# Six moves in the written-out order of an attention kernel: first set's parts, third batch's statistics, chunk 30's unit, two stores

## The chip, the cores and the metric

The kernel runs on one core of one Trainium2 chip. Its time is device microseconds (us) of one execution; lower is better. Everything is float32 in and out; some products are done in pieces on a faster format (below).

## The reference

Group norm, single-head attention over 1024 positions, projection, residual, for 4 batches:

```python
B, C, H, W = x.shape                          # 4, 128, 32, 32;  N = H*W = 1024
h = _group_norm(x, w, b)                      # 8 groups of 16 channels, over 16 x 1024 values
q = einsum('oc,bcn->bon', qw, h) + qb;  k, v likewise
attn = softmax(einsum('bcn,bcm->bnm', q, k) / sqrt(C), axis=-1)     # 4 x 1024 x 1024
out = einsum('bnm,bcm->bcn', attn, v)
out = einsum('oc,bcn->bon', pw, out) + pb
return x + out
```

## The kernel before

The weights of query and key are multiplied once (`wa`), and so are those of value and projection (`wpv`). A batch then needs one projection `g` of the normalised input `h` (`project_g`, two halves), the scores g against h, and value tiles `v` with the projection already in them (`value_tiles`, three groups of 3, 3 and 2 tiles). Products of large weight are split into a rounded part and a remainder (`h_hi`, `h_lo`, `g_hi`, `g_lo`, `p_hi`, `p_lo`, `v_hi`, `v_lo`) and summed from three matmuls.

The queries are 32 **chunks** of 128, eight for each batch. One loop over c = 0 to 31 (a **step** each) is written out on every engine, and each engine works through its own list in order, held back by semaphores alone.

- TensorE (PE) in step c: `scores(c)` into one of two PSUM halves; then the steps' extras; then `value_unit(c - 8)`, a quarter of the work of an older set.
- VectorE (DVE): `drain_scores(c)` takes the scores out of PSUM (L804), then `transpose_blocks(c - 1)` (L813).
- ScalarE (ACT): `exponentials(c)` (L620), with copies and roundings ahead of it and behind it.
- GpSimd (POOL): the remainders `v_lo` (L969), `p_lo` (L976), `h_lo`, biases and residuals.
- SyncE (SP) issues the DMAs: `move_set(n)` is 16 DMAs that carry a set's 32x32 blocks to their places in `pT`; `spread_rows(n)` spreads the softmax denominators; `store_set(n)` writes results.

Chunks form nine **sets** (`SETS = 2, 4, 4, 4, 4, 4, 4, 4, 2`); set 6 is chunks 22 to 25, set 7 is 26 to 29. Sets 1 to 7 go through the move, and their value work is a unit per chunk number: unit m of set n is `moved_unit`. Those in `SPLIT_UNITS` run as three matmuls of 256 columns per tile on `p_hi` and `p_lo` (L442 to L444), so they wait for ACT's `round_probs` (L638) and POOL's `split_probs` (L976). The first set (chunks 0, 1) and the last (30, 31) are transposed on PE instead (`transpose_probs`, L498), copied out as `pair_T` by ACT and DVE, and need no move. The first set's value work is four parts (`first_set_part`, L412), each in the step that `FIRST_SET_STEPS` names. Chunks 30 and 31 have a unit each, `last_chunk_unit` (L423).

The statistics of batch 2 (the third) are made on the way: ACT sums (`channel_means`, L592 to L595, after the exponentials of step 6; `channel_squares`, L599 to L602, after those of step 7) and raises `chan_ready`. Then PE multiplies by the deviation matrix (`group_deviations`, L303), DVE makes `cvar` and `neg_mean` (`channel_vars`, L752 and L753), PE averages (`group_vars`, L308), DVE makes `gvar` (`group_var`, L759), and POOL goes on from there. `turn_rden(1)` in step 10 (L396) waits for that `gvar`, since both use the PSUM bank A0. In steps 8 to 10 PE's lists are:

```python
# step 8:  scores(8), value_tiles(1, 1), group_deviations(2)
# step 9:  scores(9), project_g(1, 1), group_vars(2), first_set_part(3)
# step 10: scores(10), value_tiles(1, 2), turn_rden(1), value_unit(2)
```

ACT in step 10: `copy_v(1, 2)` (L610, waits for `value_tiles(1, 2)`), `copy_rows(1)`, `exponentials(10)`, then `round_probs` for units (1,2) and (1,3), that is units 4 and 5. PE reaches unit 4 in step 12.

After the loop PE's list is units 24, the transposes of chunk 31, unit 25, two `broadcast_rden`, units 26, 27, chunk 30's unit, units 28, 29, chunk 31's unit. Every unit raises `part_done` by one, and DVE's closing operations wait for counts of it. SP's list in its last rounds is move 6, spread 6, store 4, move 7, store 5, store 6, then chunk 30, set 7, chunk 31.

Of the kernel before, what the change touches and what calls it, by code (L numbers as in the profile page):

```python
# [18 lines left out]

SETS = (2, 4, 4, 4, 4, 4, 4, 4, 2)  # L20

FIRST_SET_STEPS = (4, 5, 6, 9)
FIRST_DIVIDED = 11
LAG = 8

TURN_STEPS = (3, 10, 11, 15, 19, 23, 27)
ROW_STEPS = (4, 10, 12, 15, 20, 23, 28)

DEVIATION_STEPS = (0, 8, 16)
VARIANCE_STEPS = (1, 9, 17)  # L30

CHANNEL_STEPS = (6, 7)

# [5 lines left out]
def build(nc, x, vectors, weights, out):  # L39
# [28 lines left out]
    with ExitStack() as ctx:  # L68
# [158 lines left out]
        def unit_end(r):  # L227

            n, u = SPLIT_UNITS[r]
            return FIRST[n] + u + 1  # L230

        def blocks_view(n):
            return blocks[:, n % 2, 0:SETS[n] * N].rearrange("p (j t c q) -> p j t c q", j=NQ, t=KT, c=SETS[n])
# [3 lines left out]
        @block.sync  # L237
        def _(sp):
            def move_set(n):
                sp.wait_ge(blocks_ready, FIRST[n + 1] - SETS[0])  # L240
                if n == 2:
                    sp.wait_ge(chan_ready, 3)
                if n > 2:
                    sp.wait_ge(part_done, FIRST[n - 1])
                for a in range(NQ):
                    for j in range(NQ):
                        sp.dma_start(moved_view(n)[Q * j:Q * (j + 1), a].rearrange("p t n -> p (t n)"),
                                     blocks_view(n)[Q * a:Q * (a + 1), j].rearrange("p t c q -> p (t c q)"))\
                          .then_inc(moved[n % 2][a], 16)

            def spread_rows(n):
                sp.wait_ge(rows_stored[n % 2], 16 * (n // 2 + 1))
                if n > 1:
                    sp.wait_ge(out_ready, n - 1)
                sp.dma_start(rden_bc[:, n % 2, 0:P * SETS[n]], row_store[n:n + 1, 0:P * SETS[n]].to_broadcast([P, P * SETS[n]]))\
                  .then_inc(rows_spread[n % 2], 16)

            def store_set(n):
                if n < SPREAD_BY_DMA:
                    sp.wait_ge(out_ready, n + 1)  # L260
                else:
                    sp.wait_ge(tail_out_ready, 3)
                at = P * FIRST[n]
                while at < P * (FIRST[n] + SETS[n]):
                    b, first = at // N, at % N
                    width = min(N, first + P * (FIRST[n] + SETS[n]) - at) - first
                    sp.dma_start(out[b, :, first:first + width], xb[:, b, first:first + width]).then_inc(stored, 16)
                    at += width

            def store_chunk(d):  # L270
                sp.wait_ge(tail_out_ready, (2, 4)[d])
                cs = slice(P * (CH - 2 + d), P * (CH - 1 + d))
                sp.dma_start(out[L, :, cs], xb[:, L, cs]).then_inc(stored, 16)

            for f in range(HALVES):
                cs = slice(BANK * f, BANK * (f + 1))
                sp.dma_start(x_sb[:, 0, cs], x[0, :, cs]).then_inc(x0_loaded[f], 16)
            sp.wait_ge(x0_loaded[0], 16)
            sp.dma_start(x_sb[:, 1, :], x[1]).then_inc(x1_loaded, 16)
            sp.dma_start(x_sb[:, 2:B, :], x[2:B].rearrange("b c n -> c b n")).then_inc(xs_loaded, 16)  # L280
            spread_rows(0)
            move_set(1)
            spread_rows(1)
            for n in range(2, LS):
                move_set(n)
                if n < SPREAD_BY_DMA:
                    spread_rows(n)
                store_set(n - 2)
            store_set(LS - 2)
            store_chunk(0)  # L290
            store_set(LS - 1)
            store_chunk(1)
            sp.wait_ge(stored, 16 * (NS + 1 + sum(crosses(n) for n in range(NS))))

        @block.tensor
        def _(pe):
# [119 lines left out]

            def last_chunk_unit(d):
                for f in range(HALVES):
                    pe.wait_ge(pair_ready[f], SETS[0] + SETS[LS])
                pe.wait_ge(v_ready, VP * B)  # L420
                pe.wait_ge(rowmin_ready, STEPS)
                for t in range(KT):
                    last = pe.matmul(chunk_sums[d], v[:, L % 3, t, :], pair_T[:, t, d, :], start=(t == 0), stop=(t == KT - 1))  # L423
                last.then_inc(part_done, 1)
# [89 lines left out]
            for c in range(STEPS):  # L514
                b, i = c // CH, c % CH

                late = i - 1 if b == 0 else i
                scores(c)
                if c == DEVIATION_STEPS[0]:
                    group_deviations(1)  # L520
                if late == 0:
                    value_tiles(b, 1)
                if late == 1:
                    project_g(b, 1)
                if late == 2:
                    value_tiles(b, 2)
                if c in DEVIATION_STEPS[1:]:
                    group_deviations(DEVIATION_STEPS.index(c) + 1)
                if c in VARIANCE_STEPS:
                    group_vars(VARIANCE_STEPS.index(c) + 1)  # L530
                if c in TURN_STEPS:
                    turn_rden(TURN_STEPS.index(c))
                if i == 6 and b < L:
                    project_g(b + 1, 0)
                if i == 7 and b < L:
                    value_tiles(b + 1, 0)
                if c - 2 in range(SETS[0]):
                    transpose_probs(c - 2)
                if c > DIRECT:
                    transpose_probs(c - 1)  # L540
                if c in FIRST_SET_STEPS:
                    first_set_part(FIRST_SET_STEPS.index(c))
                if c >= LAG + SETS[0]:
                    value_unit(c - LAG)
            value_unit(STEPS - LAG)
            transpose_probs(STEPS - 1)
            for m in range(STEPS - LAG + 1, FIRST[LS - 1]):
# [2 lines left out]
            broadcast_rden(LS)  # L550
            value_unit(FIRST[LS - 1])
            value_unit(FIRST[LS - 1] + 1)
            value_unit(DIRECT)
            value_unit(FIRST[LS - 1] + 2)
            value_unit(FIRST[LS - 1] + 3)
            value_unit(DIRECT + 1)
# [173 lines left out]
        def _(dve):  # L730
# [89 lines left out]
                dve.reciprocal(rden[:, n % 2, 0:SETS[n]], den[:, n % 2, 0:SETS[n]]).then_inc(rden_ready, 1)  # L820

            def divide(n):
                dve.wait_ge(part_done, FIRST[n] + SETS[n])
                if n < SPREAD_BY_DMA:
                    dve.wait_ge(rows_spread[n % 2], 16 * (n // 2 + 1))
                else:
                    dve.wait_ge(bc_ready, n - SPREAD_BY_DMA + 1)
                by_rden = rden_bc[:, n % 2, 0:P * SETS[n]]
                if n == 0:
                    dve.tensor_tensor(by_rden, sums[n], by_rden, ALU.mult).then_inc(normed_ready, 1)  # L830
                else:
                    by_rden = by_rden.rearrange("p (c a q) -> p a c q", c=SETS[n], a=NQ)
                    dve.tensor_tensor(by_rden, sums[n].rearrange("p (a c q) -> p a c q", a=NQ, c=SETS[n]), by_rden, ALU.mult)\
                       .then_inc(normed_ready, 1)

            def finish_last_chunk(d):
                dve.wait_ge(part_done, (STEPS - 3, STEPS)[d])
                dve.wait_ge(bc_ready, 2)
                by_rden = rden_bc[:, LS % 2, P * d:P * (d + 1)]
                dve.tensor_tensor(by_rden, chunk_sums[d], by_rden, ALU.mult).then_inc(chunk_normed, 1)  # L840
                dve.wait_ge(chunk_normed, d + 1)
                dve.wait_ge(xb_ready, B)
                xs = xb_flat[:, P * (DIRECT + d):P * (DIRECT + d + 1)]
                dve.tensor_tensor(xs, by_rden, xs, ALU.add).then_inc(tail_out_ready, 1)

            def finish_last_moved(part):
                n = LS - 1
                dve.wait_ge(part_done, FIRST[n] + 2 if part == 0 else STEPS - 1)
                dve.wait_ge(bc_ready, 1)
                by_rden = rden_bc[:, n % 2, 0:P * GC].rearrange("p (c a q) -> p a c q", c=GC, a=NQ)[:, 2 * part:2 * (part + 1)]  # L850
                dve.tensor_tensor(by_rden, last_sums[part].rearrange("p (a c q) -> p a c q", a=2, c=GC), by_rden, ALU.mult)\
                   .then_inc(last_normed, 1)
                dve.wait_ge(last_normed, part + 1)
                dve.wait_ge(xb_ready, B)
                xs = xb_flat[:, columns(n)].rearrange("p (c a q) -> p a c q", c=GC, a=NQ)[:, 2 * part:2 * (part + 1)]
                dve.tensor_tensor(xs, by_rden, xs, ALU.add).then_inc(tail_out_ready, 1)
# [34 lines left out]
            for c in range(STEPS):  # L891
                b, i = c // CH, c % CH
                late = i - 1 if b == 0 else i
                if c - 1 in DEVIATION_STEPS:
                    channel_vars(DEVIATION_STEPS.index(c - 1) + 1)
                if c - 1 in VARIANCE_STEPS:
                    group_var(VARIANCE_STEPS.index(c - 1) + 1)
                if i == 3 and b < L:
# [150 lines left out]
```

## Time and profile before

| what | value |
|---|---|
| median of 3 runs | 134.87 us (134.65 to 138.57) |
| the profiled execution, its own time | 134.62 us |
| its span, first to last instruction | 132.9 us |
| PE busy | 124.7 us, 94% of the span |
| DVE, ACT, POOL busy | 98.6 (74%), 84.9 (64%), 69.7 us (52%) |
| chain that ended last, share of PE | 80% |

The span is what the trace shows; the 1.7 us between it and the execution's own time lie outside the instructions. A row of the timeline gives start, duration, engine, line and operation, and in brackets how long the engine stood idle before it and what ended that. Matmuls overlap: the next starts some 0.1 to 0.2 us before the last one's record ends, so lengths of work on PE are read best from start to start.

### The profile page before, as it was taken

How to read it: one execution, taken by the hardware profiler on the slowest of the kernel's cores; microseconds unless marked ns; L12 is line 12 of the kernel's file. 1: busy time of each engine (PE TensorE's matmuls, PEld its weight loads, DVE VectorE, ACT ScalarE, POOL GpSimd, SP SyncE). 2: the span in 40 equal slices, each digit the busy share in tenths (PEclk: the TensorE clock that was granted, in tenths of full speed). 3: DMA queues.
4: the chain of work that ended last, by engine and by line, in shares of the span. 5: the costliest groups of instructions: out<-in, count | busy, mean ns of one | idle time of the engine just before them, and what ended most of it. 6: DMA issues, size and time to landing. Idle time of an engine off the chain costs nothing.

```text
span 132.9 us, 2364 instructions
## 1 busy us (share of the span) xinstructions
PE 124.7 (94%) x767; PEld 110.2 (83%) x767; DVE 98.6 (74%) x159; ACT 84.9 (64%) x149; POOL 69.7 (52%) x51
## 2 busy tenths in 40 slices
PE   5899999998699999999999999999999999699991
PEld 5897887886587889999898888898888999698991
DVE  0577878999969878989699999756987898130421
ACT  4055588768967996968756999678595369412000
POOL 5044015950006798696656696866749329923000
PEclk9999999999999999999999999999999999999999
DMA  4970000023896398899684898699738896897502
GB/s 129 286 297 0 0 5 0 0 42 81 201 215 138 122 213 205 190 239 213 167 195 125 199 215 185 198 215 222 184 142 197 204 210 221 197 212 165 178 20 99
DMA packets 9712, 21.01 MB, mean 158 GB/s; under 512 B 2378, under 2 KB 4196, under 8 KB 9700
## 3 DMA queue, kind: packets, MB, share of 16 engines
q1 hardware_dynamic: 8960, 20.59, 61.4%
q10 hardware_dynamic: 740, 0.28, 0.8%
q8 instruction: 6, 0.10, 0.3%
q14 instruction: 6, 0.05, 0.1%
HBM read 4.07 MB, written 2.11 MB: 46 GB/s over the span
## 4 chain that ended last, share of the span: by engine, by line
PE 80%; issue 6%; DVE 4%; DMA 3%; ACT 2%; POOL 2%; SPq 0%; POOLq 0%
PE ACC L471 16%; PE S L384 10%; PE S L385 9%; PE S L388 9%; PE ACC L442 6%; PE A L364 5%; PE ACC L444 5%; PE ACC L443 5%; PE S L423 3%; DMA x_sb<-x 3%; PE S L328 2%; POOL p_lo L976 2%; PE ACC L412 2%; DVE s_sb L804 1%; PE ACC L498 1%
## 5 line engine op out<-in xcount | busy, mean ns | idle before, releaser
L804 DVE TENSOR_SCALAR_CACHE_REDUCE s_sb<-S,row_term 128x1024 f32<-128x1024 f32 x32 | 40.9, 1278 | 12.3 <-PE S L388 12.0
L620 ACT ACTIVATE s_sb<-s_sb,rowmin 128x1024 f32<-128x1024 f32 x32 | 36.9, 1154 | 11.1 <-DVE s_sb L804 9.0
L976 POOL TENSOR_TENSOR p_lo<-pT,p_hi 128x1024 fp32r<-128x1024 f32 x14 | 33.4, 2394 | 11.5 <-ACT p_hi L638 11.5
L813 DVE STREAM_TRANSPOSE blocks<-s_sb 128x1024 f32<-128x1024 f32 x28 | 34.7, 1240 | 0.3
L384 PE MATMUL S<-h_hi,g_hi 128*128 128x512 f32 x64 | 27.7, 433 | 0.3 <-issue 0.3
L471 PE MATMUL ACC<-pT,v 128*128 128x128 f32 (+1 forms) x160 | 26.5, 317 | 0.0
L385 PE MATMUL S<-h_lo,g_hi 128*128 128x512 f32 x64 | 25.1, 393 | 0.0
L471 PEld LDWEIGHTS ACC<-pT,v 128*128 128x128 f32 x160 | 23.1, 191 | 2.1
L388 PE MATMUL S<-h_hi,g_lo 128*128 128x512 f32 x64 | 19.8, 391 | 0.0
L442 PE MATMUL ACC<-p_hi,v_hi 128*128 128x256 f32 x56 | 16.4, 293 | 1.2 <-POOL p_lo L976 1.1
L443 PE MATMUL ACC<-p_lo,v_hi 128*128 128x256 f32 x56 | 15.7, 281 | 0.0
L444 PE MATMUL ACC<-p_hi,v_lo 128*128 128x256 f32 x56 | 15.7, 281 | 0.0
L638 ACT CAST p_hi<-pT 128x1024 fp32r<-128x1024 f32 x14 | 14.4, 1039 | 1.3 <-DMA pT<-blocks 1.1
L388 PEld LDWEIGHTS S<-h_hi,g_lo 128*128 128x128 f32 x64 | 12.0, 188 | 2.8
L939 POOL TENSOR_TENSOR rstd<-gvar,minus_half 128x1 f32<-128x1 f32 x4 | 2.2, 553 | 22.5 <-DVE gvar L759 22.5
L384 PEld LDWEIGHTS S<-h_hi,g_hi 128*128 128x128 f32 x64 | 12.1, 189 | 2.0 <-issue 0.5
L969 POOL TENSOR_TENSOR v_lo<-v,v_hi 128x1024 fp32r<-128x1024 f32 x4 | 9.5, 2384 | 7.9 <-ACT v_hi L628 7.9
L385 PEld LDWEIGHTS S<-h_lo,g_hi 128*128 128x128 f32 x64 | 12.1, 189 | 1.6
L442 PEld LDWEIGHTS ACC<-p_hi,v_hi 128*128 128x128 f32 x56 | 10.5, 188 | 2.0 <-issue 1.7
L443 PEld LDWEIGHTS ACC<-p_lo,v_hi 128*128 128x128 f32 x56 | 10.6, 189 | 0.3
L444 PEld LDWEIGHTS ACC<-p_hi,v_lo 128*128 128x128 f32 x56 | 10.6, 189 | 0.0
L364 PEld LDWEIGHTS A<-wpv,h 128*128 128x128 f32 x64 | 8.6, 190 | 2.4 <-issue 1.7
(110 smaller groups left out, 172.5 us busy)
## 6 DMA issues: line engine op xcount, KB each, us to landing
pT<-blocks SPq DMA_DIRECT2D x112, 128.0 KB, 2.4
rden_bc<-row_store SPq DMA_DIRECT2D x6, 256.0 KB, 3.7
x_sb<-x SPq DMA_DIRECT2D x1, 1024.0 KB, 5.9
out<-xb SPq DMA_DIRECT2D x4, 256.0 KB, 3.1
out<-xb SPq DMA_DIRECT2D x7, 128.0 KB, 3.0
x_sb<-x SPq DMA_DIRECT2D x2, 256.0 KB, 3.0
x_sb<-x SPq DMA_DIRECT2D x1, 512.0 KB, 3.8
w_in<-weights ACTq DMA_DIRECT2D x2, 128.0 KB, 3.6
```

The costliest lines, as they stand in the source:

```text
L364: last = pe.matmul(A1[:, PW1 * u:PW1 * (u + 1)], h[:, P * t:P * (t + 1)], wpv[:, 0:PW1], start=True, stop=True)
L384: pe.matmul(S[:, c % 2, ks], g_hi[:, qs], h_hi[:, b % 2, ks], start=True, stop=False)
L385: pe.matmul(S[:, c % 2, ks], g_hi[:, qs], h_lo[:, b % 2, ks], start=False, stop=False)
L388: last = pe.matmul(S[:, c % 2, ks], g_lo[:, qs], h_hi[:, b % 2, ks], start=False, stop=True)
L442: pe.matmul(to, v_hi[:, t, :], p_hi[:, r % 2, w, :], start=(t == 0), stop=False)
L443: pe.matmul(to, v_hi[:, t, :], p_lo[:, r % 2, w, :], start=False, stop=False)
L444: last = pe.matmul(to, v_lo[:, t, :], p_hi[:, r % 2, w, :], start=False, stop=(t == KT - 1))
L471: last = pe.matmul(to, v[:, b % 3, t, :], probs[:, :, t, :], start=(t == 0), stop=(t == KT - 1))
L620: act.activation(s_sb[:, c % 3, :], s_sb[:, c % 3, :], ACT.Exp, bias=rowmin[:, c % CH:c % CH + 1], scale=-1.0, accum_out=den[:, n % 2, k:k ...
L804: dve.tensor_scalar(s_sb[:, c % 3, :], S[:, c % 2, :], row_term[:, b % 2, i:i + 1], None, ALU.add, ALU.min, accum_out=rowmin[:, i:i + 1]). ...
L813: dve.transpose(blocks_view(n)[:, :, :, k, :].rearrange("p j t q -> p t j q"), s_sb[:, c % 3, :].rearrange("p (t j q) -> p t j q", t=KT, j ...
L976: pool.tensor_tensor(lo, probs, hi.bitcast(F32), ALU.subtract).then_inc(p_lo_ready, 1)
```

## The change

- `FIRST_SET_STEPS` goes from (4, 5, 6, 9) to (5, 6, 7, 9). In step 7 `value_tiles(1, 0)` now stands behind that step's part.
- `group_deviations(2)` goes from the end of step 8 to just behind `scores(9)`; its `group_vars(2)` goes behind the first set's last part in step 9. DVE's `channel_vars` keeps its steps through a constant of its own. In step 10 `value_tiles(1, 2)` goes behind `value_unit(2)`.
- Chunk 30's unit goes ahead of unit 24. It now waits for three copied pairs instead of all four, and the counts of `part_done` behind it are adjusted.
- Stores 4 and 5 are issued behind move 7.

```diff
-FIRST_SET_STEPS = (4, 5, 6, 9)
+FIRST_SET_STEPS = (5, 6, 7, 9)
-DEVIATION_STEPS = (0, 8, 16)
+DEVIATION_STEPS = (0, 9, 16)
+CHANNEL_VAR_STEPS = (1, 9, 17)
...
-            return FIRST[n] + u + 1
+            return FIRST[n] + u + (2 if FIRST[n] + u >= STEPS - LAG else 1)
...
-                store_set(n - 2)
-            store_set(LS - 2)
+                if n < LS - 2:
+                    store_set(n - 2)
+            for n in range(LS - 4, LS - 1):
+                store_set(n)
...
-                    pe.wait_ge(pair_ready[f], SETS[0] + SETS[LS])
+                    pe.wait_ge(pair_ready[f], SETS[0] + d + 1)
...
                 scores(c)
-                if c == DEVIATION_STEPS[0]:
-                    group_deviations(1)
+                if c in DEVIATION_STEPS[:2]:
+                    group_deviations(DEVIATION_STEPS.index(c) + 1)
...
-                if late == 2:
+                if late == 2 and b != 1:
                     value_tiles(b, 2)
-                if c in DEVIATION_STEPS[1:]:
-                    group_deviations(DEVIATION_STEPS.index(c) + 1)
-                if c in VARIANCE_STEPS:
+                if c == DEVIATION_STEPS[2]:
+                    group_deviations(3)
+                if c in VARIANCE_STEPS and b != 1:
                     group_vars(VARIANCE_STEPS.index(c) + 1)
...
-                if i == 7 and b < L:
+                if i == 7 and 0 < b < L:
                     value_tiles(b + 1, 0)
...
                     first_set_part(FIRST_SET_STEPS.index(c))
+                if i == 7 and b == 0:
+                    value_tiles(1, 0)
+                if c == VARIANCE_STEPS[1]:
+                    group_vars(2)
                 if c >= LAG + SETS[0]:
                     value_unit(c - LAG)
+                if late == 2 and b == 1:
+                    value_tiles(1, 2)
+            value_unit(DIRECT)
             value_unit(STEPS - LAG)
...
-            value_unit(DIRECT)
             value_unit(FIRST[LS - 1] + 2)
...
-                dve.wait_ge(part_done, FIRST[n] + SETS[n])
+                dve.wait_ge(part_done, FIRST[n] + SETS[n] + (1 if n == LS - 2 else 0))
-                dve.wait_ge(part_done, (STEPS - 3, STEPS)[d])
+                dve.wait_ge(part_done, (STEPS - LAG + 1, STEPS)[d])
-                dve.wait_ge(part_done, FIRST[n] + 2 if part == 0 else STEPS - 1)
+                dve.wait_ge(part_done, FIRST[n] + 3 if part == 0 else STEPS - 1)
```

## Rows read from the trace of the kernel before

**Rows 1.** The page, TensorE's granted clock in 40 slices of the span

```profile
PEclk9999999999999999999999999999999999999999
```

**Rows 2.** Timeline of PE, steps 4 to 12: start, us, engine, line, operation

```profile
23.45 1.10 PE L412 MATMUL ACC<-pair_T,v 128*128 128x256 f32 x4 [0.38 <-issue]
...
31.58 0.91 PE L364 MATMUL A<-wpv,h 128*128 128x129 f32 x6 [0.47 <-DVE g_lo L786]
...
33.71 0.83 PE L364 MATMUL A<-wpv,h 128*128 128x129 f32 x6
35.71 0.38 PE L303 MATMUL A<-chan,deviation 128*128 128x1 f32 x2 [1.17 <-ACT chan L602]
35.95 0.48 PE L384 MATMUL S<-h_hi,g_hi 128*128 128x512 f32 x1
...
37.41 0.40 PE L340 MATMUL A<-h_hi,wa_hi 128*128 128x512 f32 x1
...
40.84 0.68 PE L364 MATMUL A<-wpv,h 128*128 128x129 f32 x4
41.36 0.27 PE L396 MATMUL A<-ident,rden 128*4 128x128 f32 x1
41.47 1.89 PE L471 MATMUL ACC<-pT,v 128*128 128x256 f32 x8
43.01 0.58 PE L384 MATMUL S<-h_hi,g_hi 128*128 128x512 f32 x1
...
47.82 0.28 PE L442 MATMUL ACC<-p_hi,v_hi 128*128 128x256 f32 x1
```

**Rows 3.** Timeline of DVE, steps 5 to 10

```profile
25.95 1.28 DVE L804 TENSOR_SCALAR_CACHE_REDUCE s_sb<-S,row_term 128x1024 f32<-128x1024 f32 x1 [0.19 <-PE S L388]
...
36.28 0.18 DVE L752 SCALAR_TENSOR_TENSOR cvar<-A,chan 128x1 f32<-128x1 f32 x1
...
37.61 1.28 DVE L804 TENSOR_SCALAR_CACHE_REDUCE s_sb<-S,row_term 128x1024 f32<-128x1024 f32 x1 [1.08 <-PE S L388]
...
40.61 0.14 DVE L759 TENSOR_SCALAR gvar<-A 128x1 f32<-128x1 f32 x1
```

**Rows 4.** Timeline of ACT, steps 7 to 10

```profile
35.45 0.20 ACT L602 ACTIVATE chan<-chan_sums 128x1 f32<-128x1 f32 x1
...
41.56 0.37 ACT L610 COPY v<-A 128x256 f32<-128x256 f32 x1 [0.44 <-PE A L364]
...
43.78 1.98 ACT L638 CAST p_hi<-pT 128x1024 fp32r<-128x1024 f32 x2
```

**Rows 5.** Timeline of POOL, units 4 and 5, and units 24 and 25

```profile
44.89 4.75 POOL L976 TENSOR_TENSOR p_lo<-pT,p_hi 128x1024 fp32r<-128x1024 f32 x2 [0.90 <-ACT p_hi L638]
...
112.53 4.70 POOL L976 TENSOR_TENSOR p_lo<-pT,p_hi 128x1024 fp32r<-128x1024 f32 x2
```

**Rows 6.** Timeline of PE, behind the loop

```profile
111.99 1.95 PE L471 MATMUL ACC<-pT,v 128*128 128x128 f32 x16
115.04 0.36 PE L442 MATMUL ACC<-p_hi,v_hi 128*128 128x256 f32 x1 [1.10 <-POOL p_lo L976]
...
123.00 1.95 PE L423 MATMUL S<-pair_T,v 128*128 128x128 f32 x16
124.78 3.62 PE L471 MATMUL ACC<-pT,v 128*128 128x256 f32 x16
```

**Rows 7.** Timeline of ACT, the copy of chunk 30's pair

```profile
112.65 0.58 ACT L660 COPY pair_T<-A 128x512 f32<-128x512 f32 x1
```

**Rows 8.** Timeline of SP: start, length of issuing, line

```profile
30.76 10.12 SPq L247 DMA_DIRECT2D pT<-blocks  x16
...
110.77 11.25 SPq L247 DMA_DIRECT2D pT<-blocks  x16
122.06 1.58 SPq L267 DMA_DIRECT2D out<-xb  x3
```

**Rows 9.** Issues by line, set moves from 108 us on: us from issue to landing

```profile
DMA to landing us min/median/max: 2.3/2.7/3.2
```

More of the change, by code:

```diff
@@ L893, in _ @@
                 late = i - 1 if b == 0 else i
-                if c - 1 in DEVIATION_STEPS:
-                    channel_vars(DEVIATION_STEPS.index(c - 1) + 1)
+                if c in CHANNEL_VAR_STEPS:
+                    channel_vars(CHANNEL_VAR_STEPS.index(c) + 1)
                 if c - 1 in VARIANCE_STEPS:
```

## The prediction

> **What bounds the kernel now.** I read the busy times first: TensorE is busy 124.7 of 132.9 us, and the chain that ended last is 80% its own. So an edit pays only where TensorE stands still, and only if the time isn't given back at its next wait. The second view is therefore TensorE's timeline with the brackets. It has four places that the edits touch. In step 4 the first set's first part waits 0.38 us. In step 7 the value tiles of batch 1 wait 0.47 us for DVE's `g_lo`. In step 8 the deviation product waits 1.17 us for ACT's `chan` [rows 2]. Behind the loop unit 24 waits 1.10 us for POOL's `p_lo` [rows 6]. Between unit 4 in step 12 and the end of the loop TensorE goes from one operation to the next nearly without a bracket. So I treat the kernel as a front (to unit 4 at 47.82 us), a middle of fixed length, and a tail. The third view is the timelines of DVE, ACT and POOL, to see what feeds unit 4 and what else is late in the tail.
>
> **Part 1, the front: parts a step later, deviations behind scores 9.** The question is when unit 4 starts, and the answer needs two chains: when TensorE gets there, and when `p_lo` gets there.
>
> Steps 4 to 7. Without a part in step 4, scores 5 ends earlier, and DVE's drain of step 5 loses its idle 0.19 us [rows 3], with the handover some 0.25. From there DVE drains and transposes without pause until `g_lo`, so the value tiles of step 7, which wait for that `g_lo`, start 0.25 earlier: 31.58 becomes 31.33 [rows 2]. TensorE, which no longer loses 0.38 in step 4, simply waits longer here (about 1.1 us instead of 0.47). Moving the parts thus yields 0.25 us, not 0.38 + 0.47.
>
> Steps 8 and 9. The second value tiles start at 33.71 and are recorded for 0.83; less the 0.17 by which a follower overlaps (part 2) they take 0.66, to 34.37; then comes the wait, and scores 9 start at 35.95 [rows 2]. Now scores 9 follow the tiles at once: 34.37 - 0.25 = 34.12. They take 37.41 - 35.95 = 1.46 [rows 2], so the deviation product can start at 35.6. `chan` is written at 35.65 [rows 4] and rides on the same copy and exponential as before, so it comes 0.25 earlier, at 35.4. The wait is gone. DVE is free for `cvar` at 36.28 - 0.25 = 36.03, as before less the 0.25, and behind it stands drain 9, queued after the added wait. In the kernel before this drain waited 1.08 us for scores 9 [rows 3]. That idle time goes, since scores 9 end before `cvar` is even made; drain 9 starts at about 36.3 instead of 37.61, 1.3 earlier. The drain, a transpose and `g_lo` lead on to `gvar`, so `gvar` starts at 40.61 - 1.3 = 39.3 [rows 3] and is done at 39.45. The cost of the product between scores 9 and the projection is a tenth of a microsecond and lies in DVE's shadow.
>
> Step 10. TensorE is done with scores 10 before that, and `turn_rden` waits for `gvar` with nothing in front of it any more. From `gvar` to the start of `p_lo` of unit 4 the sum goes: handover 0.1; the turn 41.47 - 41.36 = 0.11; unit 2, now ahead of the tiles, 43.01 - 41.47 = 1.54 [rows 2]; from the start of the last two value tiles to their copy on ACT 41.56 - 40.84 = 0.72 [rows 2, 4]; from that copy through the rows and the exponential to the rounding, 43.78 - 41.56 = 2.22 [rows 4]; from the rounding to `p_lo` 44.89 - 43.78 = 1.11 [rows 4, 5]. That is 5.80, so `p_lo` starts at 45.25. From the start of a `p_lo` to the start of its unit takes 115.04 - 112.53 = 2.51 [rows 5, 6]. Unit 4 can start at **47.76, against 47.82 before**: the reorder makes `gvar` 1.3 earlier, and it puts unit 2 (1.54) between `gvar` and the exponential on ACT, which is queued behind the copy of those tiles.
>
> TensorE itself gets there earlier: scores 11 would start at 39.45 + 0.1 + 0.11 + 1.54 + 0.45 (two tiles, two thirds of the 0.66) = 41.65 instead of 43.01, and 4.81 later [rows 2], at 46.5, it stands before unit 4 and waits 1.3 us. So nearly all that the front wins is paid back at one new wait, which no bracket of the present trace shows because POOL is just in time. Unit 5 follows: its `p_lo` is done 4.75 us after 45.25, at 50.0, and the unit starts a unit and a pass of scores behind unit 4, 3.0 us by the lengths above, at 50.8, which leaves 0.8. Net for the front: 0.06 us, bounds from +0.4 (handovers) to -1.3 (unit 4 is not held back at all).
>
> **A rule against this new wait.** The trace grants the full level, 2.4 GHz, in every slice, though TensorE stands still for 1.17 and 1.10 us in it [rows 1, 2, 6]. The Trainium skill says that TensorE's clock is gated by default and activity releases it ("TensorE: Matmul & The Clock Gate", What's actually happening); it would let four waits in steps 7 to 12, the longest 1.3 us, end at 1.2 GHz. The mechanism would be a stretch at half rate behind the wait. A pair of scores and unit is 1.46 + 1.54 = 3.0 us here [rows 2], so one such pair at half rate adds 3.0.
>
> **Part 2, the tail: chunk 30's unit ahead of unit 24.** The unit is only moved, so TensorE's work stays the same and it fills the wait. Unit 23 starts at 111.99 and is recorded for 1.95; a follower starts 0.17 before such an end (123.00 + 1.95 against 124.78), so at 113.77 [rows 6]. What the moved unit needs is there: ACT's copy ends at 113.23 [rows 7], DVE's beside it at the same time, and DVE's copy stands in its list behind the drain of the last scores. It takes 124.78 - 123.00 = 1.78, to 115.55; unit 24 starts 0.51 later than 115.04 and all that followed chunk 30's old place 1.78 - 0.51 = **1.27 us earlier** [rows 6]. The `p_lo` of unit 25 is done at 117.23 [rows 5], ahead of the unit's 117.9. DVE finishes chunk 30 between the two halves of set 7, with time in hand.
>
> What is late next is set 7's move. Unit 28 needs the last quarter of it; it would be asked for at 124.78 - 1.27 - 0.06 = 123.45. The move starts when chunk 29's blocks are made, at 110.77, and is issued in 11.25 us here, 10.12 in the first [rows 8]. Its last DMA lands 2.3 to 2.7 us after its issue [rows 9], which itself lies 0.6 before the end. That gives 122.6 to 124.1. I take no wait, nearer to the shorter end, since the stores no longer go ahead of this move and only issues held up for a microsecond make the long case; the long end costs 0.65.
>
> **Part 3, the two stores.** Store 4 is two DMAs ahead of move 7, about 1.05 us by the 1.58 for three [rows 8]; I count nothing for taking it away, since move 7 has a condition of its own, the blocks of chunk 29. Had the store held it up, the move would start up to 1.05 earlier, which only takes chance from rival (b). Behind the move stand five store DMAs instead of three; three take 1.58 [rows 8], so five take 2.6 and end near 124, while chunk 30's store is wanted at about 125 and the last near 129.6. At nothing, as long as SP stays that far ahead; if not, the last store would slip by 0.4 a DMA.
>
> **Sum.** -0.06 - 1.27 = -1.33 us. The profiled execution goes from 134.62 to 133.3, and the median, 0.25 above it, from 134.87 to 133.5. The change of `unit_end` and the other counts follow the new order and cost nothing.
>
> **The rivals.** (a) The front is kept: unit 4 isn't held by `p_lo`, because ACT's list catches up in its idle time. For it speaks that ACT and POOL are busy only 64% and 52%; against it, that the chain above has no slack in it. It gives 133.5 - 1.3 = 132.2. (b) The last move isn't in time, and unit 28 waits up to 0.65: 134.2. For it speaks the 11.25. (c) Slower than before: the tiles behind unit 2 cost more than the statistics win. Every tenth that `gvar` comes later than 39.45 delays unit 4 by a tenth, and the middle hands it on to the end. The point from which it decides is a `gvar` at 40.8: from there on the tail's 1.27 is used up. If `chan` comes so late that DVE's drain 9, now queued behind `cvar`, gains nothing, and the 0.6 of round trip to TensorE and back is added, `gvar` is 1.9 later: 133.5 + 1.9 = 135.4. Against it: `chan` comes from ACT's own list, which nothing in steps 5 to 8 delays. (d) The clock falls for one pair: 133.5 + 3.0 = 136.5; against it the full clock after every present wait [rows 1]. (e) The tail does nothing, since its unit isn't ready when unit 23 ends: 134.8; the copies' ends half a microsecond before speak against it.
>
> **How the numbers follow.** The forecast, 133.0 to 134.0, has 0.62; (a) 0.12; (b) 0.12; (c) 0.08; (d) 0.02; (e) 0.04. The likeliest gives 133.5. The range leaves out most of (c), (d), and a corner of the others: 132.1 to 134.9. Two per cent, about what a measurement of this kernel tells from no change, is 2.7 us, so below 132.17 counts as faster: a part of (a), 0.05. Slower begins at 137.57, beyond (d) on average: 0.01. Within lies 0.94.
>
> **What the profile after would show.** Brackets at 23.45 and before L303 gone; a longer one before L364 in step 7; one of about 0.4 before L396 in step 10; `gvar` near 39.4; a bracket of about 1.3 before L442 near 47.8, ended by POOL's `p_lo`; chunk 30's unit (L423) near 113.7, with no bracket before unit 24; unit 28 near 123.4. I am wrong if unit 4 starts more than half a microsecond away from 47.8, or if unit 28 or unit 24 has a bracket of its own.

## The result, and the profile after

The changed kernel takes 134.03 us (median of 18 runs, 133.5 to 138.0) against 134.85 us in as many runs of the kernel before. The ratio is 0.9949, 95% interval 0.9937 to 0.9960, so the change makes the kernel 0.7 us faster, 0.5%; that is clear of no change, and under the two per cent that the prediction took as faster. (Medians are over all runs, 0.8 us apart here; ratios, here and below, leave out the few runs that took some 3% longer, such as the 138.0.) The forecast was 133.5 us, 1.33 us faster. The profiled execution took 134.02 us, its span is 132.3 us, and TensorE is busy for 124.9 us of it, 0.2 more than before. The clock row is again full in every slice.

TensorE's timeline of the changed kernel, the front, with the rows that answer to [rows 2] (lines have moved by four on TensorE, ten on DVE, ACT and POOL, and two on SP):

```profile
24.28 1.02 PE L416 MATMUL ACC<-pair_T,v 128*128 128x256 f32 x4
...
31.28 0.91 PE L368 MATMUL A<-wpv,h 128*128 128x129 f32 x6 [0.77 <-DVE g_lo L796]
...
34.01 0.47 PE L388 MATMUL S<-h_hi,g_hi 128*128 128x512 f32 x1
...
35.49 0.31 PE L307 MATMUL A<-chan,deviation 128*128 128x1 f32 x2
...
39.41 0.27 PE L400 MATMUL A<-ident,rden 128*4 128x128 f32 x1
39.53 1.96 PE L475 MATMUL ACC<-pT,v 128*128 128x256 f32 x8
41.34 0.61 PE L368 MATMUL A<-wpv,h 128*128 128x129 f32 x4
...
47.83 0.36 PE L446 MATMUL ACC<-p_hi,v_hi 128*128 128x256 f32 x1 [1.27 <-POOL p_lo L986]
```

The waits of steps 4 and 8 are gone; scores 9 start at 34.01 instead of 35.95. The wait of step 7 has grown from 0.47 to 0.77 in its bracket, and step 9 has a small one of 0.20 before its projection. The last row holds the bracket of 1.27 us that was not there before, and unit 4 starts at 47.83 where it started at 47.82.

What comes between, on DVE, ACT and POOL of the changed kernel ([rows 3], [rows 4] and [rows 5] answer to these):

```profile
36.00 0.18 DVE L762 SCALAR_TENSOR_TENSOR cvar<-A,chan 128x1 f32<-128x1 f32 x1
...
39.16 0.15 DVE L769 TENSOR_SCALAR gvar<-A 128x1 f32<-128x1 f32 x1
```

```profile
41.98 0.37 ACT L620 COPY v<-A 128x256 f32<-128x256 f32 x1 [2.25 <-PE A L368]
...
44.20 1.98 ACT L648 CAST p_hi<-pT 128x1024 fp32r<-128x1024 f32 x2
```

```profile
45.30 4.75 POOL L986 TENSOR_TENSOR p_lo<-pT,p_hi 128x1024 fp32r<-128x1024 f32 x2 [2.76 <-ACT p_hi L648]
```

`gvar` is 1.45 us earlier than before (39.16 against 40.61), but ACT then stands idle for 2.25 us until the last value tiles come, and the rounding and `p_lo` are 0.4 later than before.

TensorE's timeline behind the loop ([rows 6]) and SP's ([rows 8]), changed kernel:

```profile
112.05 1.95 PE L475 MATMUL ACC<-pT,v 128*128 128x128 f32 x16
113.83 1.95 PE L427 MATMUL S<-pair_T,v 128*128 128x128 f32 x16
115.54 0.36 PE L446 MATMUL ACC<-p_hi,v_hi 128*128 128x256 f32 x1
...
119.99 3.62 PE L475 MATMUL ACC<-pT,v 128*128 128x256 f32 x16
124.15 3.69 PE L475 MATMUL ACC<-pT,v 128*128 128x256 f32 x16 [0.54 <-DMA pT<-blocks]
127.68 1.95 PE L427 MATMUL S<-pair_T,v 128*128 128x128 f32 x16
```

```profile
110.82 11.33 SPq L249 DMA_DIRECT2D pT<-blocks  x16
122.20 2.57 SPq L269 DMA_DIRECT2D out<-xb  x5
125.09 0.33 SPq L275 DMA_DIRECT2D out<-xb  x1
128.79 0.33 SPq L269 DMA_DIRECT2D out<-xb  x1
130.31 0.33 SPq L275 DMA_DIRECT2D out<-xb  x1
```

Chunk 30's unit fills the wait ahead of unit 24, which has no bracket any more. But unit 28 stands until 124.15 for the last quarter of set 7's move; without that it would follow unit 26 by 3.46 us, the time from unit 26 to the next operation in [rows 6] (119.54 to 123.00), at 123.45. That is 0.70 of the 1.27 us given back. SP is done issuing that move at 110.82 + 11.33 = 122.15, and unit 28 starts 2.00 us later. The five stores are issued by 124.8, before chunk 30's is wanted.

### The profile page after: what moved, and what is told of

Its sections match the earlier page's. It is cut to its first block, busy times and chain, and to the rows that moved or that the text cites. A ratio compares the mean times of both kernels' runs of the same rounds, so it can differ in the third digit from the quotient of the medians.

```text
span 132.3 us, 2364 instructions
## 1 busy us (share of the span) xinstructions
PE 124.9 (94%) x767; PEld 110.3 (83%) x767; DVE 98.3 (74%) x159; ACT 84.6 (64%) x149; POOL 69.9 (53%) x51
## 4 chain that ended last, share of the span: by engine, by line
PE 70%; SPq 8%; DVE 7%; issue 6%; ACT 3%; POOL 2%; DMA 2%; ACTq 0%; POOLq 0%; DVEq 0%
PE ACC L475 12%; PE S L388 9%; PE S L389 8%; PE S L392 8%; SPq L249 8%; PE A L368 6%; PE S L332 5%; PE ACC L446 4%; PE ACC L448 4%; PE ACC L447 4%; DVE blocks L823 3%; DVE s_sb L814 2%; DMA pT<-blocks 2%; POOL p_lo L986 2%; PE S L427 1%
```

## The experiments

The theory (A) was the prediction's, with rival (b) (set 7's move isn't in time) now seen to have come true: the front gives nothing net because the value tiles behind unit 2 hold `p_lo` of unit 4; the tail gives 1.3 less what unit 28 waits. The runs of one group shared a chip.

**Part alone: the tail.** The kernel before with chunk 30's unit moved, with its shorter wait and the counts that go with it.

```diff
+            value_unit(DIRECT)
             value_unit(STEPS - LAG)
...
             value_unit(FIRST[LS - 1] + 1)
-            value_unit(DIRECT)
```

> The kernel before with one part of the change: chunk 30's unit ahead of unit 24, and the counts that go with it. Theory A (the front gives nothing net, the tail gives all): 0.6 us faster than before, ratio 0.995 to 0.996, the whole change's; unit 24 without a bracket near 115.5 us, and unit 28 waiting about 0.6 us for the last quarter of set 7's move. Rival B (the front does give something that the tail loses again): 0.3 us or less, ratio above 0.9975.

Measured: 133.83 us, ratio 0.9917 (0.9896 to 0.9938). A's 0.995 to 0.996 lies outside that: the gain is 1.1 us and not 0.6, and no smaller than the whole change's. TensorE's closing rows show why:

```profile
113.80 1.95 PE L423 MATMUL S<-pair_T,v 128*128 128x128 f32 x16
115.51 0.36 PE L442 MATMUL ACC<-p_hi,v_hi 128*128 128x256 f32 x1
...
119.97 7.37 PE L471 MATMUL ACC<-pT,v 128*128 128x256 f32 x32
127.18 1.95 PE L423 MATMUL S<-pair_T,v 128*128 128x128 f32 x16
```

Units 26 to 29 run in one group here with no bracket. They take 127.18 - 119.97 = 7.21 us, only 0.29 more than the 2 x 3.46 that they need; in the changed kernel they take 7.69. The move was issued in 10.89 us instead of 11.33. SP is done with it at 121.69, and unit 28 starts 1.97 us later, at 123.66. So the gain of the tail stands, and its loss depends on the move.

**Part alone: the front.** The changed kernel with the tail and the stores put back.

> The changed kernel with chunk 30's unit and the two stores put back: the front's reorder alone. Theory A: no difference, ratio 0.999 to 1.001; TensorE waits 1.3 us before unit 4, which starts at 47.8 us, and 1.1 us again before unit 24. Rival B: 0.3 to 0.6 us faster, ratio below 0.998.

Measured: 134.97 us, ratio 1.0000 (0.9982 to 1.0018), as A had it. TensorE waits 1.3 us before unit 4 and 1.1 before unit 24, 2.4 us together. In this profile all times behind the first scores are 0.4 us late (those start at 12.13 instead of 11.72 us); from there to unit 4 (48.22) it is 36.09 us, against 36.10 before.

**The stores back.** `store_set(n - 2)` in every round of SP's loop again, the rest as changed.

> The changed kernel with stores 4 and 5 back in their old places. Theory A (the stores neither hold nor slow set 7's move; its length comes from one DMA whose issuing is held up by a microsecond, which happens either way): the same as the changed kernel, 0.6 to 0.7 us faster than before. Rival C (two DMAs ahead of the move slow its first issues): unit 28 starts 0.4 us later, ratio 0.998.

Measured: 134.08 us, ratio 0.9946 (0.9925 to 0.9967): the same as the changed kernel. Rival C's 0.998 lies outside, and moving the stores does nothing that can be measured. Only store 4 changes its place at all: store 5 stood behind move 7 in the kernel before too, as the first of the three DMAs at 122.06 in [rows 8]. The profiled execution was the slowest of its ten (134.84 us); unit 28 waited 1.10 us in it, and its move has this DMA:

```profile
L249 SPq DMA_DIRECT2D pT<-blocks x1: 2194/2194/2194, 118.9 to 118.9; - x1
```

It is one issue of 2.19 us, where nearly all others take 0.59; another of this move takes 0.80.

**The value tiles back.** The changed kernel, with the last two tiles of batch 1 ahead of the turn and unit 2, as they were.

```diff
-                if late == 2 and b != 1:
+                if late == 2:
                     value_tiles(b, 2)
...
-                if late == 2 and b == 1:
-                    value_tiles(1, 2)
```

> The changed kernel with the last two value tiles of batch 1 back ahead of the turn and unit 2 in step 10. Theory A (those tiles behind unit 2 hold ACT's exponential of step 10, and with it the p_lo of unit 4, which gives back all that the statistics win): ACT copies the tiles near 40.0 instead of 41.98 us, p_lo of unit 4 starts at 44.0 instead of 45.30 (by then the move of set 1 is the next limit), unit 4 starts at 46.4 to 46.6 and the bracket before it falls under 0.3 us; the middle carries it to the end, 1.2 to 1.4 us faster than the changed kernel, ratio to before 0.985 to 0.987. Rival D (POOL or the move of set 1 holds unit 4 anyway): 0.5 us or less faster than the changed kernel, ratio above 0.991.

Measured: 132.86 us, ratio 0.9841 (0.9811 to 0.9870): 1.2 us faster than the changed kernel by the medians, 1.4 to 1.5 by the ratios. Its ACT, POOL and TensorE:

```profile
40.32 0.37 ACT L618 COPY v<-A 128x256 f32<-128x256 f32 x1 [0.38 <-PE A L368]
...
42.80 2.00 ACT L646 CAST p_hi<-pT 128x1024 fp32r<-128x1024 f32 x2 [0.16 <-DMA pT<-blocks]
```

```profile
43.92 4.77 POOL L984 TENSOR_TENSOR p_lo<-pT,p_hi 128x1024 fp32r<-128x1024 f32 x2 [1.17 <-ACT p_hi L646]
```

```profile
46.59 0.28 PE L446 MATMUL ACC<-p_hi,v_hi 128*128 128x256 f32 x1
```

Where the two tiles stand accounts for the front's loss. ACT's idle time goes from 2.25 to 0.38 us, `p_lo` starts at 43.92 (expected 44.0), and unit 4 has no bracket. The rounding now waits 0.16 us for set 1's move, but TensorE doesn't wait for it. Rival D is out.

**The changed kernel again**, as the reference of the second group.

> The changed kernel once more, beside the next three on one chip, so that small differences can be read against it. Theory A: ratio to before 0.992 to 0.996, with times spread over half a microsecond or more, since how long one held-up DMA of set 7's move takes differs from run to run and unit 28 waits for it.

Measured: 134.21 us, ratio 0.9937 (0.9909 to 0.9965), as A had it; eight of the nine times lie between 133.42 and 134.45. Unit 28 has a bracket of 0.54 again, and the tenth DMA of the move is issued in 1.97 us.

**The last rows behind unit 27.** The two `broadcast_rden` after units 26 and 27.

> The changed kernel with the six transposes that broadcast the last denominators behind units 26 and 27 instead of ahead of them. TensorE's work is the same; 0.65 us of it moves into the place where unit 28 waits for the last quarter of set 7's move. Theory A (what the tail lacks of its 1.3 us is that DMA's landing): unit 28 starts as before with no bracket or under 0.3 us, 0.3 to 0.6 us faster than the changed kernel. Rival E (something else behind unit 28 sets the end, the stores behind the move or DVE's closing work): no difference.

Measured: 134.13 us, ratio 0.9919 (0.9888 to 0.9949), not told apart from the changed kernel. The expectation was reasoned wrongly: the rows stood ahead of unit 28 already, so nothing was moved into its wait. What the run does show is that unit 28 starts at nearly the same time in either order ahead of it:

```profile
119.45 3.69 PE L475 MATMUL ACC<-pT,v 128*128 128x256 f32 x16
122.98 0.82 PE L406 MATMUL S<-ident,rden 128*128 128x128 f32 x6
124.27 3.69 PE L475 MATMUL ACC<-pT,v 128*128 128x256 f32 x16 [0.47 <-DMA pT<-blocks]
```

Units 26 and 27 come 0.7 us earlier than in the run beside it, and unit 28 at 124.27 instead of 124.33. So set 7's move sets its start. Whether something behind unit 28 holds the end as well (rival E) it doesn't decide.

**Part alone: the first set's parts.** The kernel before with `FIRST_SET_STEPS = (5, 6, 7, 9)` and step 7's value tiles behind the part.

> The kernel before with the first set's parts a step later and the value tiles of step 7 behind that step's part, and nothing else. Theory A: the wait of step 4 goes and the one of step 7 grows; DVE comes 0.25 us earlier and so does everything up to unit 4, since the reorder of step 10 isn't in it: 0.2 to 0.3 us faster than before, ratio 0.998. Rival F (the parts alone are worth the brackets that they remove, 0.38 and 0.47): 0.8 us faster, ratio 0.994. Rival G: nothing, ratio 1.000.

Measured: 134.61 us, ratio 0.9971 (0.9953 to 0.9990): about 0.4 us faster, in the direction of A; A's 0.998 lies in the interval, rivals F and G outside it. The wait of step 7 is 0.77 us, `gvar` starts at 40.38 instead of 40.61, and unit 4 at 47.58 instead of 47.82. So the trace bears out 0.24 at unit 4, but not at the end: TensorE is still 0.25 ahead at 94.98, the next unit's `p_lo` starts at 93.73 (92.95 before), and at 96.29 TensorE is 0.02 behind (96.27 before). The span is 132.9 us in both profiles, so what of the 0.4 us is the parts' isn't shown.

**Both repairs.** Tiles back and the rows behind unit 27.

> Both repairs: the value tiles of step 10 back ahead of unit 2, and the last denominators' transposes behind unit 27. Theory A: the two waits are in series on TensorE, so the gains add: 1.5 to 1.9 us faster than the changed kernel, about 132.4 us, ratio to before 0.981 to 0.984; no bracket of more than 0.3 us between step 8 and the last unit.

Measured: 132.10 us, ratio 0.9781 (0.9754 to 0.9809), faster than A's 0.981 to 0.984. The interval lies just below those of both runs with the tiles alone (0.9841, and 0.9834 below), so the second repair may add something here. It isn't shown, since those ran on other chips and the profiles end alike: the last unit starts at 125.59 here and at 125.54 in the second run with the tiles alone. No bracket of over 0.3 us stands between step 8 and the end. Its held-up DMA is 1.34 us, and the move 10.76.

**The last quarter issued from ACT.** Behind `exponentials(31)` in ACT's list.

```diff
-                for a in range(NQ):
+                for a in range(NQ - 1 if n == LS - 1 else NQ):
...
                 exponentials(c)
+                if c == STEPS - 1:
+                    act.wait_ge(blocks_ready, FIRST[LS] - SETS[0])
+                    act.wait_ge(part_done, FIRST[LS - 2])
+                    for j in range(NQ):
+                        act.dma_start(moved_view(LS - 1)[Q * j:Q * (j + 1), NQ - 1].rearrange("p t n -> p (t n)"), ...)
```

> The changed kernel with the last four of set 7's sixteen move DMAs issued from ACT, behind its last exponential near 114.5 us, in place of SP. Theory A (unit 28 waits for the end of a row of DMAs whose length is their issuing, sixteen of 0.63 us and one held up for a microsecond more): SP is done with its twelve near 119.7, the last quarter lands before 120.5, unit 28 has no bracket and starts at 123.45; 0.4 to 0.7 us faster than the changed kernel, ratio to before 0.989 to 0.991. Rival H (the transfers themselves are the limit, so that two queues only share them): the last of them lands no earlier than 123, the bracket stays over 0.3 us.

Measured: 134.41 us, ratio 0.9953 (0.9928 to 0.9978): nothing gained, and in the profiled execution unit 26 waits instead of unit 28.

```profile
119.50 0.82 PE L406 MATMUL S<-ident,rden 128*128 128x128 f32 x6
121.40 1.97 PE L475 MATMUL ACC<-pT,v 128*128 128x256 f32 x8 [1.08 <-DMA pT<-blocks]
```

SP's twelve DMAs of this move now take this long to land, against a median of 2.3 us in the changed kernel and 2.7 in [rows 9]:

```profile
L249 SPq DMA_DIRECT2D pT<-blocks x12: 507/592/1622, 111.0 to 118.2; - x12
DMA to landing us min/median/max: 2.2/4.3/5.9
```

And the DMA engines while both queues are at work, 113 to 116 us (busy times of the engines, clock, DMA share, GB/s); first this kernel, then the changed one:

```profile
113.00:116.00 3.00, 3.00 (x29) 3.00 (x28) 0.61 (x2) 1.60 (x3) 3.00 (x2) 1.00 0.94 247
```

```profile
113.00:116.00 3.00, 3.00 (x29) 3.00 (x29) 0.44 (x2) 1.43 (x3) 3.00 (x2) 1.00 0.90 209
```

The DMA engines were 90% busy with one queue; in this stretch a second adds 18% of throughput, and the median time to landing nearly doubles. Theory A fell here: the last DMA from SP is issued at 118.2 and lands 4.6 us later, so the row's length isn't its issuing alone, and rival H is nearer. Part of the failure is the order. ACT issued its four DMAs while its copy and its last exponential were still to run, at 112.94 and not at 114.5:

```profile
112.88 0.58 ACT L670 COPY pair_T<-A 128x512 f32<-128x512 f32 x1
112.94 0.58 ACTq L727 DMA_DIRECT2D pT<-blocks  x1
113.36 1.15 ACT L630 ACTIVATE s_sb<-s_sb,rowmin 128x1024 f32<-128x1024 f32 x1
```

So they went in ahead of SP's fifth to eighth DMA. Unit 26 needs the first eight; the eighth was issued at 115.35 and took 5.91 us to land.

**Tiles back, and the quarter from ACT.**

> The changed kernel with the value tiles of step 10 back ahead of unit 2, and the last quarter of set 7's move issued from ACT. Theory A: both losses gone, 1.8 us faster than the changed kernel, about 132.1 us, ratio to before 0.979 to 0.982. Rival H: as the tiles alone, ratio 0.984.

Measured: 132.15 us, ratio 0.9811 (0.9789 to 0.9833). A's 0.979 to 0.982 fits, and rival H's 0.984 lies just outside; but H's claim is that this equals the tiles alone, which the next run measures beside it.

**Tiles back, again.**

> The changed kernel with only the value tiles of step 10 back ahead of unit 2, once more, to be read beside the one before. Theory A: ratio 0.982 to 0.986, 0.3 us or more behind the kernel that also has the quarter issued from ACT.

Measured: 132.52 us, ratio 0.9834 (0.9814 to 0.9855). The repair is confirmed. The gap of 0.37 us to the run just above is of the size that A asked for, but the two intervals overlap, so the quarter from ACT isn't shown to help.

**The tail alone, again.**

> The kernel before with chunk 30's unit moved alone, once more. Theory A: ratio 0.991 to 0.995, the same as the whole change within 0.3 us; what differs between them is only how long the held-up DMA of set 7's move is and when it comes. Rival I (the front's reorder costs 0.3 us or more in the whole change): ratio 0.992 or less with all times under 134.0.

Measured: 133.78 us, ratio 0.9932 (0.9911 to 0.9953). Rival I's condition isn't met (two of the times are 134.25 and 134.19), and A's 0.991 to 0.995 is. Still, both medians of the tail alone lie 0.2 us or more under those of the changed kernel. The two never ran beside each other on one chip, and the intervals overlap, so a small cost of the front's reorder is neither shown nor excluded.

**What sets the wait of unit 28.** For each profile: the issuing of the longest DMA of set 7's move, and what units 26 to 29 take beyond 6.92 us (start of the last unit less start of unit 26, less 0.65 where the rows stand between).

| kernel | longest issue, us | beyond 6.92, us |
|---|---|---|
| stores back | 2.19 | 1.33 |
| changed, again | 1.97 | 0.76 |
| changed | 1.90 | 0.77 |
| rows behind 27 | 1.90 | 0.78 |
| tiles back | 1.64 | 0.51 |
| tail only | 1.41 | 0.29 |
| tiles and rows | 1.34 | 0.23 |
| tiles again | 1.32 | 0.25 |
| tail again | 1.31 | 0.15 |

A longer held-up DMA goes with a longer wait, nearly one for one up to 1.90 us. What unit 28 waits for is the end of the row: in the five profiles where it has a bracket (changed, changed again, stores back, rows behind 27, tiles back), it starts 2.0 us after SP is done issuing the move. That could be read before the change. By [rows 8] SP is done at 110.77 + 11.25 = 122.02, and the last of those DMAs landed at 124.0 (issued at 121.4, 2.6 us to landing). Unit 28 started at 124.78 then, with 0.8 us to spare; asked for at 123.45 it would have waited 0.6.

The changed kernel's own row, and what else the DMA engines carried while it was held up (queues in the stretch 116.3 to 118.4 us: packets, MB, share):

```profile
L249 SPq DMA_DIRECT2D pT<-blocks x1: 1902/1902/1902, 116.4 to 116.4; - x1
DMA to landing us min/median/max: 3.7/3.7/3.7
```

```profile
q1 hardware_dynamic: 108, 0.26, 53.2%
q8 instruction: 1, 0.02, 4.6%
```

One packet of queue q8, "instruction", falls into the stretch; there are six in the whole run. The same holds for all thirteen profiles in which a DMA of this move takes 1.3 us or more to issue: one such packet lies at its start, or up to half a microsecond ahead. In the fourteenth, with the tiles back and the quarter from ACT, the packet comes at 119.2, when this move has been issued, and no issue is that long:

```profile
L249 SPq DMA_DIRECT2D pT<-blocks x12: 507/594/805, 109.5 to 116.6; - x12
```

So the two go together in every profile. That the packet causes the hold-up isn't shown; nor would it explain all, since the kernel before also has an issue of 1.06 us at 112.6, with no such packet near.

## Why the prediction was right, and where it was off

- **Reading TensorE's brackets as a front, a fixed middle and a tail** held here. From unit 4 to unit 23 TensorE takes 64.22 us in the changed kernel and 64.17 before. It isn't a law: with the parts alone it takes 64.45.
- **The parts a step later are worth 0.25 us.** Right up to unit 4: 31.28 for the forecast 31.33, and the run of this part alone has unit 4 0.24 earlier, though its profile doesn't end earlier.
- **`gvar` 1.3 earlier, `p_lo` at 45.25, unit 4 at 47.76 with a new wait of 1.3.** Right to a tenth for `p_lo` (45.30), unit 4 (47.83) and the wait (1.27), in part by luck: `gvar` came 0.14 earlier than forecast (39.16 against 39.3), and from the start of unit 2 to that of the tiles it took 1.81 us (39.53 to 41.34) where the sum has 1.54. The small wait of 0.4 before the turn, in the prediction's list of signs, doesn't stand in TensorE's rows. The front alone measured nothing, and putting the tiles back made 1.2 to 1.5 us appear, with ACT's idle time gone. That shows the cause as the prediction named it. Its bound of -1.3 for an unheld unit 4 is what the tiles back delivered.
- **Rival (d), the clock at half rate for a pair**, did not come: the granted clock stays at the full level, 2.4 GHz, in every slice, through the 1.27 us wait and the others, as the trace of before suggested. The rule of the Trainium skill that it was set beside ("TensorE: Matmul & The Clock Gate", What's actually happening), that the clock is gated by default and activity releases it, made no difference to this kernel.
- **The moved unit is worth 1.27.** Right as work on TensorE: 113.83, 115.54 and no bracket, against 113.77 and 115.55.
- **"I take no wait" for unit 28** is the term that was mis-sized. Forecast 0, with 0.65 at the long end; the changed kernel's profile has 0.70. That is rival (b), which had a chance of 0.12, and it is nearly the whole of the gap between 1.33 and the measured 0.7 us. It took the time out of the stretch 133.0 to 134.0, which had 0.62, into (b)'s 134.2: 134.85 times the ratio is 134.2, and the median is 134.03. By the prediction's own last sentence, a bracket before unit 28 means that it was wrong there. The time lies inside the wider stretch, 132.1 to 134.9, as (b) was allowed for there. The step that failed is the choice of the shorter end. It leans on the first move's 10.12 us, while this very move's row says 11.25; by that row its own sum gives 123.7 to 124.1, a wait of 0.25 to 0.65. The ground given failed too: without the stores ahead of it the move is 11.33 us long, and the one held-up issue that makes the long case comes in every profile where SP issues all sixteen.
- **The stores at nothing**: right, by the run with them back.

Still open is why that DMA is held up for 1.3 us in some kernels and 1.9 or more in others, and what the instruction packet beside it fetches and for which engine. Changing the length of SP's list to move it wasn't tried. Open too is whether the front's reorder costs a little: neither run of the tail alone was slower than the whole change.

## What to carry to other kernels

An operation put behind another on one engine is late for every engine that reads it: before a product is moved down a list, follow its reader's own list to the next thing the first engine waits for. Removing the front's two waits (0.38 and 1.17 us) was worth nothing while two small tiles held up another engine's queue, and 1.2 us or more once they were back. And when work fills the last idle place before the end, the transfer for the work behind it is asked for earlier by as much; price that transfer by its own row in the trace of before, not by a shorter relative. Here that row and the 2.0 us from the end of issuing to the last landing gave a wait of 0.6, and 0.7 came.

## What the runs showed of the hardware

One of the sixteen DMAs in set 7's move takes 1.3 to 2.2 us to issue in every profile where SP issues them all, where the others mostly take 0.59. A packet of the instruction queue lies beside it each time. Where the packet came after the move, no issue took over 0.81 us. Unit 28, when it waits, starts 2.0 us after SP has issued the last of the row. A second issuing queue beside a first that keeps the DMA engines 90% busy raised throughput from 209 to 247 GB/s, and the median time to landing from 2.3 us (16 DMAs of 128 KB in a row) to 4.3. A DMA written behind an activation in ACT's list was issued before that activation ran (112.94 against 113.36), since no semaphore tied it to that activation.
